# The squared-ReLU hand-over between ScalarE and VectorE in the up tiles of a gated cross-attention block

## The reference, cut to what matters

```python
h = jax.nn.relu(jnp.einsum('bsh,hi->bsi', hidden_states, up_w)) ** 2   # 1024 -> 2048
shared_out = jnp.einsum('bsi,ih->bsh', h, down_w)                      # 2048 -> 1024
x_latent = jnp.einsum('bsh,hl->bsl', hidden_states, fc1_w)             # 1024 -> 512
moe_out = jnp.einsum('bsl,lm->bsm', x_latent, expert_w) * routing_sum
routed_out = jnp.einsum('bsl,lh->bsh', moe_out, fc2_w)
return _layernorm(shared_out + routed_out, ln_gamma, ln_beta)
x = x + jnp.tanh(g_ffn[0]) * (that)
```

## Time and profile before

| what | value |
|---|---|
| median of three executions | 1007.84 us |
| the profiled execution's own time | 1008.68 us |
| span of that execution (first to last instruction) | 1006.5 us |
| mean granted TensorE clock | 0.985 |
| TensorE matmuls busy | 948.0 us, 94% |
| VectorE busy | 484.1 us, 48% |
| ScalarE busy | 323.2 us, 32% |
| GpSimd busy | 324.5 us, 32% |
| TensorE idle 205.29 to 213.90 us, before the first shared product | 8.61 us |

### The profile page before, as it was taken

How to read it: one execution, slowest core, us unless ns; L and a number is a source line. 1 busy time by engine, 2 the same in 40 slices (tenths; PEclk the granted TensorE clock), 3 DMA queues, 4 the chain that set the end, 5 groups by cost and what they waited for, 6 DMA issues and landing times.

```text
span 1006.5 us, 12367 instructions
## 1 busy us (share of the span) xinstructions
PE 948.0 (94%) x4562; PEld 441.6 (44%) x4562; DVE 484.1 (48%) x845; ACT 323.2 (32%) x441; POOL 324.5 (32%) x149
## 2 busy tenths in 40 slices
PE   2898799969999999999999999999999999999995
PEld 1346544434444444444444444444444444444442
DVE  6366588896466244455574244455574222221112
ACT  2457777553322112233332112233332112211111
POOL 4250224045954233033763333033763200001110
PEclk9899999979999999999999999999999999999998
DMA  8797797323234354423225244422225222200001
GB/s 347 206 312 262 296 384 279 113 80 105 85 96 139 106 180 152 143 90 84 58 93 144 99 160 152 141 92 84 59 90 145 77 94 102 84 1 7 15 21 42
DMA packets 63999, 131.28 MB, mean 130 GB/s; under 512 B 35266, under 2 KB 35394, under 8 KB 62658
## 3 DMA queue, kind: packets, MB, share of 16 engines
q1 hardware_dynamic: 62786, 126.07, 38.7%
q10 hardware_dynamic: 1152, 4.39, 1.2%
HBM read 105.09 MB, written 19.07 MB: 123 GB/s over the span
## 4 chain that ended last, share of the span: by engine, by line
PE 81%; DVE 9%; ACT 2%; DMA 2%; issue 2%; DVEq 2%; POOL 1%; SPq 0%; ACTq 0%; POOLq 0%
PE psS L1328 31%; PE psR L1278 18%; PE psS L1278 16%; PE psR L1338 8%; PE psP L1246 5%; PE psP L1259 2%; DVE ring L1055 1%; DVE s L893 1%; DVE hid L1106 1%; DVE s L897 1%; DMA sim_scratch<-simo 1%; PE psR L1384 1%; DMA sim_side<-sim_scratch 1%; DVEq L1092 1%; ACT hid L765 1%
## 5 line engine op out<-in xcount | busy, mean ns | idle before, releaser
L1328 PE MATMUL psS<-big,hid 128*128 128x512 f16 x1536 | 337.6, 381 | 8.9 <-issue 8.6
L1328 PEld LDWEIGHTS psS<-big,hid 128*128 128x128 f16 x1536 | 150.5, 98 | 191.4 <-issue 11.7
L1278 PE MATMUL psS<-xT,ring 128*128 128x512 f16 (+1 forms) x912 | 191.7, 370 | 3.0 <-DVE xT L1001 1.7
L1278 PE MATMUL psR<-xT,ring 128*128 128x512 f16 (+1 forms) x912 | 190.0, 368 | 0.0
L1278 PEld LDWEIGHTS psS<-xT,ring 128*128 128x128 f16 x912 | 89.8, 99 | 102.5 <-issue 4.8
L1278 PEld LDWEIGHTS psR<-xT,ring 128*128 128x128 f16 x912 | 89.2, 98 | 97.2
L517 POOL TENSOR_TENSOR y<-y,lgb 128x1024 f32<-128x1024 f32 x15 | 39.3, 2617 | 251.7 <-ACT y L655 251.7
L1019 DVE SCALAR_TENSOR_TENSOR y<-psR,rw,y 128x1024 f32<-128x1024 f32 x15 | 19.2, 1282 | 140.6 <-PE psR L1338 140.6
L1338 PE MATMUL psR<-w,lgb 128*128 128x512 f16 x384 | 85.5, 379 | 0.0
L488 POOL TENSOR_TENSOR sides<-scr 128x1024 f32<-128x1024 f32 x12 | 29.3, 2440 | 141.6 <-DMA scr<-in_ctx 141.6
L507 POOL TENSOR_TENSOR ring<-f_buf,ring 128x1024 f32<-128x1024 f32 x18 | 39.2, 2177 | 100.8 <-ACT f_buf L623 68.8
(11 more groups left out here) (196 smaller groups left out, 989.0 us busy)
## 6 DMA issues: line engine op xcount, KB each, us to landing
ring<-pair_scratch SPq DMA_DIRECT2D x60, 512.0 KB, 3.4
ring<-sim_scratch SPq DMA_DIRECT2D x18, 504.0 KB
big<-in_w_up SPq DMA_DIRECT2D x8, 1024.0 KB, 13.7
out_rows<-y SPq DMA_DIRECT2D x15, 512.0 KB, 3.0
hid<-in_w_down SPq DMA_DIRECT2D x14, 512.0 KB, 7.7
big<-in_w_down SPq DMA_DIRECT2D x14, 512.0 KB, 8.2
pair_scratch<-ring SPq DMA_DIRECT2D x12, 512.0 KB, 7.0
sim_side<-sim_scratch SPq DMA_DIRECT2D x11, 504.0 KB
```

The lines of the kernel that those rows point to most:

```text
L1278: mm = pe.matmul(up_bank[t % NR][:, cols], rows[:, a, k, :], xT[:, k, b, cols], start=(k == 0 and a == 0 and b == 0), stop=(k == KB - 1 an ...
L1328: mm = pe.matmul(psS[:, HALF * h:HALF * h + HALF], hT[:, i, a, P * j:P * j + P], dn[:, i, b, HALF * h:HALF * h + HALF], start=(i == 0 and ...
```

## The change

ScalarE still takes the positive part of the bank into the buffer, and this now frees the bank. After a drain ScalarE squares the buffer into the float16 high half. VectorE waits for that, multiplies the buffer by itself in place, drains, and subtracts the high half. The scale of the positive part is 2^-23 instead of 2^-45, and a later factor is adapted. In block 0 the down rows are split later in each step (behind the tile's own work and behind `cosines`), ten stand in the up half and six in the down half, the shared product's rows each wait for their own hidden row, and `xattn` comes after 10 rows instead of 12.

```diff
-HID_SHIFT = -45
+HID_SHIFT = -23
-        DN_SPLIT = {13: (0, 2), 14: (2, 4), 15: (4, 6), 16: (6, 8), 17: (8, 10), 18: (10, 12), 19: (12, 13)}
-        DN_LATE = range(13, IT)
+        DN_SPLIT = {13: (0, 2), 14: (2, 4), 15: (4, 6), 16: (6, 8), 17: (8, 10)}
+        DN_LATE = range(10, IT)
-        XATTN_AT, XATTN_FIRST = (5, 0, 0, 0), (12, 12, 10, 6)
+        XATTN_AT, XATTN_FIRST = (5, 0, 0, 0), (10, 12, 10, 6)
 # ScalarE, up_half
-                        act.activation(buf, bank, ACT.Relu, scale=2.0 ** HID_SHIFT).then_inc(relu_rdy, 1)
+                        act.activation(buf, bank, ACT.Relu, scale=2.0 ** HID_SHIFT).then_inc(up_evac, 1)
                     if first and EARLY + t < IT:
                         act.wait_ge(*out_of(t))
                         tile_hi(EARLY + t)
-                    if first:
-                        for c in range(*DN_SPLIT.get(t, (0, 0))):
-                            dn_split_hi(c)
                     if t >= LT:
-                        act.wait_ge(sq_hid, i + 1)
-                        act.activation(hT[:, t - LT, 0, :], hbuf[:, t % 2, :], ACT.Copy).then_inc(h_hi, 1)
+                        act.drain()
+                        act.activation(hT[:, t - LT, 0, :], hbuf[:, t % 2, :], ACT.Square).then_inc(h_hi, 1)
...
+                        for c in range(*DN_SPLIT.get(t, (0, 0))):
+                            dn_split_hi(c)
 # VectorE, up_half
-                        dve.wait_ge(relu_rdy, i + 1)
-                        dve.scalar_tensor_tensor(out=hbuf[:, t % 2, :], in0=bank, scalar=0.0,
-                                                 in1=hbuf[:, t % 2, :], op0=ALU.max, op1=ALU.mult)
-                        dve.drain().then_inc(up_evac, 1)
-                        dve.drain().then_inc(sq_hid, 1)
+                        dve.wait_ge(h_hi, i + 1)
+                        dve.tensor_tensor(hbuf[:, t % 2, :], hbuf[:, t % 2, :], hbuf[:, t % 2, :], ALU.mult)
...
                     if first and EARLY + t < IT:
                         tile_lo(EARLY + t)
-                    if first and t == SCALE_T:
-                        down_scale()
-                    if first:
-                        for c in range(*DN_SPLIT.get(t, (0, 0))):
-                            dn_lo(c)
                     if t >= LT:
-                        dve.wait_ge(h_hi, i + 1)
+                        dve.drain()
                         dve.tensor_tensor(hT[:, t - LT, 1, :], hbuf[:, t % 2, :], hT[:, t - LT, 0, :],
                                           ALU.subtract).then_inc(h_rdy, 1)
                     if phase_a and t == X_T:
                         x_stats(m, 0)
+                    if first and t == SCALE_T:
+                        down_scale()
                     if phase_a and t == COS_T:
                         cosines(m)
+                    if first:
+                        for c in range(*DN_SPLIT.get(t, (0, 0))):
+                            dn_lo(c)
 # TensorE
-                    pe.wait_ge(up_evac, t - NR + 1)
+                    bank_free(0, t)          # lat_evac for latent tiles, up_evac for hidden ones
 # shared()
                     if first:
+                        pe.wait_ge(h_rdy, i + 1)
                         pe.wait_ge(dn_rdy, i + 1)
 # down_half(), j == 0
-                        pe.wait_ge(up_evac, UT * (n + 1) - 2)
-                        pe.wait_ge(h_rdy, IT * (n + 1) - 2)
+                        pe.wait_ge(up_evac, IT * (n + 1) - 2)
                         if first:
                             pe.wait_ge(w2_rdy, LT)
+                        else:
+                            pe.wait_ge(h_rdy, IT * (n + 1) - 2)
```

More of the change, by code:

```diff
@@ L212, in flamingo_block @@
         home_rdy = sem("home_rdy")
-        up_done, up_evac = sem("up_done"), sem("up_evac")
-        relu_rdy, sq_hid, h_hi, h_rdy = sem("relu_rdy"), sem("sq_hid"), sem("h_hi"), sem("h_rdy")
+        up_done, lat_evac, up_evac = sem("up_done"), sem("lat_evac"), sem("up_evac")
+        h_hi, h_rdy = sem("h_hi"), sem("h_rdy")
         l_hi = sem("l_hi")
@@ L1074, in down_scale @@
                 dve.drain()
-                dve.tensor_scalar(c_s, coef[:, 4:5], 2.0 ** -17, None, ALU.mult)
+                dve.tensor_scalar(c_s, coef[:, 4:5], 2.0 ** -16, None, ALU.mult)
                 dve.drain().then_inc(scale_rdy, 1)
@@ L1085, in up_half @@
                                                  in1=lat[:, t, 0, :], op0=ALU.mult, op1=ALU.subtract)\
-                            .then_inc(up_evac, 1)
+                            .then_inc(lat_evac, 1)
                     else:
                         i = IT * n + t - LT
-                        dve.wait_ge(relu_rdy, i + 1)
-                        dve.scalar_tensor_tensor(out=hbuf[:, t % 2, :], in0=bank, scalar=0.0,
-                                                 in1=hbuf[:, t % 2, :], op0=ALU.max, op1=ALU.mult)
-                        dve.drain().then_inc(up_evac, 1)
-                        dve.drain().then_inc(sq_hid, 1)
+                        dve.wait_ge(h_hi, i + 1)
+                        dve.tensor_tensor(hbuf[:, t % 2, :], hbuf[:, t % 2, :], hbuf[:, t % 2, :], ALU.mult)
                     for j in range(BB if phase_a else 0):
@@ L1281, in tile, with bank_free @@
                 return mm
+            def bank_free(n, t):
+                if t < NR + LT:
+                    pe.wait_ge(lat_evac, LT * n + t - NR + 1)
+                else:
+                    pe.wait_ge(up_evac, IT * n + t - NR - LT + 1)
             def first_up_half():
@@ L1302, in up_half @@
                     if t >= NR:
-                        pe.wait_ge(up_evac, UT * n + t - NR + 1)
+                        bank_free(n, t)
                     else:
@@ L1367, in down_half @@
                     else:
-                        pe.wait_ge(up_evac, UT * (n + 1))
+                        pe.wait_ge(up_evac, IT * (n + 1))
                     if not phase_a and j == BB - 1:
```

## The result

The changed kernel takes 1012.25 us (median of 16 executions, 1007.03 to 1014.53), the kernel before, run in turn with it, 1006.54 us (16 executions, 1002.03 to 1008.86). The ratio is 1.0053 with a 95% interval of 1.0038 to 1.0068: the change costs some 5.3 us. The forecast of 1007.0 and its range (to 1010.0) are both missed; "slower" had a chance of 0.15.

A forecast was written before the change was run, and what follows sets the result against it. TensorE was taken as the bound, with only its block 0 start-up waits movable: 0.8 us won less 0.2 lost in blocks 1 and 2 gives 0.6, so 1007.2 against the median, stated as 1007.0; range 1001.5 to 1010.0.

The forecast's parts named there:

- Stretch 1: Block 0, tile 4 to tile 11: VectorE turns to tile 12 at 180.7 instead of 173.9; TensorE pauses 4.4 us.
- Stretch 2: Block 0, from VectorE's turn to tile 12 to its low halves for `xattn`: 45.3 us instead of 51.2, ending at 226.0.
- 8.61 us pause: TensorE's wait in block 0 between the gates and first shared product; said to go, with 3.5 us ahead of `xattn` instead.
- 12.9 us: Most the change could win at block 0's start-up: bank wait 1.8, pause behind the gates 8.6, slow clock 2.5.
- The rest of block 0 hangs on this product and moves with it.: Block 0 behind the second sequence's shared product, forecast at 245.4 instead of 246.2: keeps the 0.8 us won.
- D: Block 0: end of VectorE's last late conversion, forecast at 233.5 where it was 228.94 before.
- What is late next: Block 0's down half: six late conversions end at 233.5, `psS` is emptied at 245.3, second sequence starts at 245.4.
- The row-by-row wait lets TensorE start at about 209: Block 0's first shared product: waiting per hidden row, ten rows take 13.0 us and end at 222.5.
- Blocks 1 to 3: No bank wait left to remove, earlier release worth nothing; blocks 1 and 2 lose about 0.1 us each ahead of `xattn`.
- The first, VectorE not late: Rival, block 0 tiles 4 to 11: multiply not held, load early; gain 4.0 to 7.5 us, likeliest 1002.8; chance 0.32.
- The second rival: Block 0, tile 15: the sum over the down rows stops TensorE for 9 us; loss 3.5 us, 1011.3; chance 0.15.
- The third, that banks alone decide: Rival, block 0 tiles 18 and 19: only the 1.77 us bank wait goes, 1006.1; chance 0.53 together with the forecast.

The follow-up runs named there:

- e4: The changed kernel without GpSimd's four additions of beta to `home` in block 0 (left out of the output); ratio to before 1.0028.
- e7: The changed kernel with two hidden-row waits instead of 16, `psS` emptied earlier by ScalarE and GpSimd's first output finished earlier in block 0; ratio to before 1.0002.
- e5: The changed kernel with two waits for hidden rows in TensorE's first shared product instead of 16; ratio to before 1.0024.
- e6: The kernel before with 16 already met waits for hidden rows added in TensorE's first shared product; ratio to before 1.0017.
- e3: The changed kernel, but VectorE multiplies the buffer by the bank again and frees the bank itself; ratio to before 1.0028.
- e8: e7 with VectorE's multiply reading the bank, as in e3; ratio to before 0.9963, median 1003.47 us.

## Why the prediction was wrong, step by step

- **Stretch 1 was right in the hold, not in the load.** The multiply is held beside GpSimd, the sum over the down rows ends at 178.58 (said 179.9), and TensorE pauses 2.87 us ahead of tile 15 (said 4.4) with a slow tile behind it (6.75 for 5.34). But the load of down row 13, from which "the sum cannot end before 178.9" came, bound nothing: it was issued at 167.09, not 168.6, ScalarE waited 0.25 us for it and had squared the row by 174.31. VectorE alone was late. ScalarE's row, then VectorE's rows of the change:

```profile
173.15 1.03 ACT L695 ACTIVATE psP<-hid 128x1024 f32<-128x1024 f32 x1 [0.25 <-DMA hid<-in_w_down]
```

```profile
138.42 2.43 DVE L1090 TENSOR_TENSOR sim_side<-sim_side 128x512 f32<-128x512 f32 x1 [2.13 <-ACT hid L684]
...
178.42 0.16 DVE L1060 TENSOR_REDUCE amx<-fro 128x1 f32<-128x16 f32 x1
...
224.51 1.22 DVE L937 TENSOR_TENSOR u_buf<-y,u_buf 128x1024 f16<-128x1024 f32 x1
...
230.80 2.48 DVE L1049 SCALAR_TENSOR_TENSOR big<-lgb,wsc,big 128x1024 f16<-128x1024 f32 x2
```

- **Stretch 2 was right in its times, in part by luck.** The low halves for `xattn` end at 225.73 (said 226.0), the late conversions at 233.28 (said 233.5), the second sequence starts at 245.08 (said 245.4). But VectorE turned to tile 12 at 178.6, not at 180.7, and needed 47.1 us from there to the low halves instead of 45.3. It was busy for 44.2 of them, where the 45.6 of before less three conversions (3.75) leave 41.8. The two errors, 2.1 early and 1.8 long, cancel. The 8.61 us pause went and came back as 2.87, 4.64 and 0.60 and as slow matmuls: of 12.9 us 1.1 were won there.
- **The step that failed:** "The rest of block 0 hangs on this product and moves with it." It does not. The third sequence hangs on `take_s` of the second, this on the store of the first output, and that on GpSimd's chain, which starts at the late conversions and not at the product. D moved from 228.94 to 233.28. The third sequence starts 44.2 us behind D, and before it started at 276.41: from D = 232.2 on it is later than before. The step "What is late next" followed D to the first `take_s` and stopped; ScalarE's high halves and GpSimd's `f_lo` behind them were the other branch, 1.3 us late. It cost the 1.1 us won, 1.0 us on top, and 1.7 us of clock. e4 and e7 show it from both sides.
- **What no step had:** the waits added to TensorE enter the prediction only by when they let it start ("The row-by-row wait lets TensorE start at about 209"); as instructions they stand at nothing, without a reason. Ahead of a loop the 16 of them cost 2.5 us (the table's last column; e5 and e6 by time 0.29% and 0.17%). The 1.22 us stall stood in the trace before, behind block 1.
- **Blocks 1 to 3** were put at 0.1 us lost in blocks 1 and 2 each; 0.4 was won in each, since the wait ahead of `xattn` went. Wrong in sign, and small.
- **The rivals.** The first, VectorE not late, is e3: its multiply is not held and its sum ends at 176.2. The rival gave 5.3 us there for the second sequence (246.2 less 176.2 + 64.7); e3's starts 4.7 earlier, 1.6 of them start-up, behind a wait of 2.32 us. The forecast of time behind it failed like the main one, by the code's place. The second rival had the right sign by another way: the pause at tile 15 is 2.87 us, not 9. The third, that banks alone decide, is out: the 1.77 us wait went and nothing was won by it.

## What to carry to other kernels

When work is moved behind a hand-over, follow every consumer of the late result down to its next meeting with the bound engine, store and buffer reuse included; here the branch that decided ran over two other engines and met TensorE 44 us later. Count added instructions on the bound engine as code as well as waits, and look at the first instructions behind each jump back for an "issue" pause before and after. A pause of 2 us on TensorE can cost nearly twice its length (2.39 us and 1.7 behind it in the change), so removing one and making two smaller ones need not be a gain.

## What the runs showed of the hardware

- One tile read as both inputs of a VectorE operation is held by GpSimd like two tiles: the multiply took up to 2.84 us and 923 ns in the mean, and with the bank as one input 689 and 693 at most. The Trainium skill (SBUF — State Buffer, "Who interferes with whom") has a VectorE instruction with two SBUF inputs contend with a GpSimd instruction that reads SBUF, and one with at most one SBUF input not; the trace agrees, for the same tile twice as well (2.59 us for the multiply of tile 11 inside GpSimd's product, 0.68 with the bank).
- Sixteen waits on TensorE ahead of a loop moved the stall behind its jump back from behind the 8th or 9th matmul to behind the 2nd, and from between 0.76 and 1.36 us (five kernels) to between 1.94 and 2.44 (five kernels), also where all of them were met (e6). By what mechanism is not shown.
- After a pause of TensorE the clock sometimes falls to 1.2 GHz and sometimes stays at 2.4, at the same place: behind the stall at the jump the next 46 matmuls took 10.10 us at a pause of 1.94 and 2.18 us, 11.79 at 2.28 and 2.34, 13.04 at 2.44. But in e8 a pause of 2.02 ahead of `xattn` already made it slow (5.75 against 4.05). What decides is open.
